# First product by row tiles, adapters with transposes three units behind and y's parts taken from PSUM

## The chip, the cores and the metric

One core of a Trainium2 chip runs the whole kernel as one program. The metric is the device time of one execution in microseconds (us). A core has TensorE (PE), which multiplies and transposes into PSUM, VectorE (DVE), ScalarE (ACT), GpSimd (POOL), which has no operand in PSUM in this kernel, and SyncE (SP), whose queue issues the DMAs here. Each engine works its own instructions off in the order written; between engines semaphores order the work.

## The reference, cut

Four sequences x of 512 x 512, everything in float32. One attention block with a two-stage network, then three adapters in a row (L1, L2, L3); for every sequence b, `stream[b]` picks one of three weight sets.

```python
q, k, v = x @ Wq, x @ Wk, x @ Wv
attn_out = softmax(q @ k.T * V ** -0.5) @ v @ Wp + bp
cms = gelu(attn_out @ cW1 + cb1) @ cW2 + cb2 + one_hot(code)
mod = gelu(concat(attn_out, cms) @ mW1 + mb1) @ mW2 + mb2
x = clip(x + cms + mod, 0, 1)
for layer in (L1, L2, L3):
    h = gelu(x @ W_down[stream] + b_down[stream]) @ W_up[stream] + b_up[stream]
    y = x + h
    x = (y - mean(y)) / sqrt(var(y) + 1e-5) * gamma[stream] + beta[stream]
```

## The kernel before

**Precision.** An operand of a product is held in two parts: the high part is the float32 value rounded to fp32r by a copy, the low part is value minus high part, rounded too. A product of two such operands takes three matmuls (high x high, high x low, low x high). ScalarE makes high parts, VectorE low ones, as a rule.

**First product** (`product(J_G, ...)`, the first of TensorE's program). G = Wq Wk^T, so that the scores are (x G) x^T. Wq and Wk arrive transposed in four row tiles of 128 each, eight DMAs of 256 KB on SP (L374). ScalarE casts each tile (L820), VectorE subtracts (L1142). TensorE computes four banks m, and for each runs over the four row tiles k, three matmuls each: 48 of 128x512. Bank 0 waits for the split of each tile k. The finished banks are cast (L781) and subtracted (L1084) into `g_w`, which the second product (x G) reads, each of its banks over all four tiles of `g_w`. In between ScalarE casts x and VectorE subtracts (L790, L1094). After that come the value product, scores, softmax and the two-stage network, which aren't changed; beside them weights of the adapters are split piece by piece (L796, L1516) and stored to DRAM.

**Adapters.** Twelve units u: layer u // 4 of sequence u % 4. A unit is, on TensorE: down (`t_down_mm`, 24 matmuls: h^T, two banks m of 512), up (`t_up_mm`, 24 matmuls: four banks `UP[i]`, rows of the sequence in the partitions), and 16 transposes of 128x128 (`t_transpose`, L756) of the normalised z back to columns of the sequence. In between:

- ScalarE: `h_gelu` (L1038, from PSUM to `hf`) and the casts of h (L1043); `z_norm` (L1028, four tiles of z in place); `y_scale` (L1052, PSUM times gamma plus beta to `yf`) and four casts of `yf` to the high part of `yT` (L1057).
- VectorE: `h_lo` (L1426, two), `z_stats`: z = UP + res (L1446), bn_stats (L1452) and bn_aggr (L1458) for four row tiles, `factors` (L1420, minus mean times rstd), `y_lo` (L1471, four, `yf` minus high part).
- GpSimd: variance plus eps (L1534) and its power -0.5, rstd (L1536), then for units 0 to 7 the result in rows, z times gamma (L1543) plus beta (L1545), four tiles each, which is the residual `res` of unit u + 4.

TensorE's program is written by slots s: down(s), up(s-1), transposes(s-2). Unit u's down reads `yT` of unit u-4, so a unit's result has two slots to become an operand. PSUM has eight banks: four are `UP`, four hold by turns down results and transposes (`down_bank`, `tr_bank`). z has two buffers, and z of unit u may be overwritten when GpSimd has read it and TensorE has transposed it. Units from `FINE` = 10 take their statistics in halves, so that normalising begins after two tiles. `y0_to_rows(b)` (L696, 16 transposes) and `y0_rows` (L1415) bring each sequence's first residual into rows, in slots 0 to 2.

SP loads in the order of its program: down weights `wd` (1 MB, L478) and up weights `wu` (1 MB, L485) of a unit, ten columns `pp` of gamma, beta and bias for each unit (L492), gamma and beta broadcast to rows `bc` (L498, L499), which waits for GpSimd's results of the unit two before.

## Time and profile before

| | us |
|---|---|
| median of 3 runs | 1217.73 |
| lowest and highest | 1216.46, 1219.93 |
| the profiled execution | 1217.09 |
| its span (first to last instruction) | 1215.0 |

| engine | busy us | share of the span |
|---|---|---|
| TensorE matmul | 1183.5 | 97% |
| VectorE | 808.1 | 67% |
| ScalarE | 565.2 | 47% |
| GpSimd | 173.3 | 14% |

GpSimd works only in about the first and the last sixth of the span. The trace gives for an instruction its start and its duration; a 128x512 matmul is listed with about 390 ns, but the next starts 227 ns after it, since they are pipelined. So a row of n matmuls covers about n x 0.227 plus the rest of the last one. "Idle before" in brackets is how long the engine had nothing, and whose instruction ended that. An interval that is spoken of as a slot goes from the first matmul of one down to the next.

### The profile page before, as it was taken

What the parts mean: (1) busy time and instruction counts of PE and PEld (TensorE: products, weight loads), DVE (VectorE), ACT (ScalarE), POOL (GpSimd) and SP (SyncE); (2) the same over time, 40 slices, a digit from 0 to 9 for tenths busy, and PEclk for the clock granted to TensorE, in tenths of its full rate; (3) what the DMA queues carried; (4) which work ended last, traced back from release to release, by engine and by line L of the source; (5) the groups of instructions that cost most, each with busy time, mean ns of one, the idle gap of its engine ahead of it and who ended that gap; (6) DMA issues with size and microseconds to landing.
All of it is one profiled execution on the core that took longest, in us unless ns stands there. A gap on an engine that the chain in (4) does not pass through costs nothing.

```text
span 1215.0 us, 15228 instructions
## 1 busy us (share of the span) xinstructions
PE 1183.5 (97%) x5312; PEld 974.9 (80%) x5312; DVE 808.1 (67%) x1461; ACT 565.2 (47%) x1068; POOL 173.3 (14%) x147
## 2 busy tenths in 40 slices
PE   7999999999999999999999999999999999999987
PEld 5888888788888788888888888878888888788776
DVE  5444395666668656565667776786665656889886
ACT  5344353563544534342435643454343343466666
POOL 1332230000000000000000000000000000578871
PEclk9999999999999999999999999999999999999999
DMA  5755452114320203020551311411111119655544
GB/s 192 266 205 174 165 178 104 53 46 162 122 96 35 96 1 104 4 101 14 201 237 52 131 61 35 174 53 52 53 52 53 52 48 364 229 168 181 175 150 162
DMA packets 51186, 145.82 MB, mean 120 GB/s; under 512 B 6420, under 2 KB 6420, under 8 KB 46886
## 3 DMA queue, kind: packets, MB, share of 16 engines
q1 hardware_dynamic: 51110, 144.84, 33.9%
q8 instruction: 43, 0.70, 0.2%
q14 instruction: 33, 0.27, 0.1%
HBM read 108.11 MB, written 36.71 MB: 119 GB/s over the span
## 4 chain that ended last, share of the span: by engine, by line
PE 79%; POOL 8%; DVE 6%; ACT 3%; issue 3%; DMA 1%; SPq 0%; POOLq 0%; ACTq 0%; DVEq 0%
PE psum L549 78%; POOL res L1543 3%; POOL res L1545 3%; ACT z L1028 1%; POOL sm L1536 1%; DVE sm L1452 1%; DVE res L1335 1%; DMA wk_raw<-wts_dram 1%; DVE res L1280 1%; ACT ring L885 0%; DVE ring L1199 0%; PE psum L756 0%; PE psum L583 0%; DVE z L1446 0%; DVE c_op L1307 0%
## 5 line engine op out<-in xcount | busy, mean ns | idle before, releaser
L549 PE MATMUL psum<-g_hl,w_hl 128*128 128x512 f32 x1536 | 351.4, 389 | 0.5 <-DVE w_hl L1258 0.4
L549 PEld LDWEIGHTS psum<-g_hl,w_hl 128*128 128x128 f32 x1536 | 288.2, 188 | 61.0 <-DVE w_hl L1258 0.8
L549 PE MATMUL psum<-a_op,ring 128*128 128x512 f32 x1344 | 319.0, 391 | 6.6 <-DVE w_t L1239 6.1
L549 PEld LDWEIGHTS psum<-a_op,ring 128*128 128x128 f32 x1344 | 253.2, 189 | 60.9 <-DVE w_t L1239 7.3
L549 PE MATMUL psum<-c_op,ring 128*128 128x512 f32 x672 | 165.1, 392 | 0.6 <-DVE c_op L1307 0.6
L549 PEld LDWEIGHTS psum<-c_op,ring 128*128 128x128 f32 x672 | 126.9, 189 | 28.4 <-DVE c_op L1307 2.0
L885 ACT CAST ring<-asum 128x256 fp32r<-128x256 f32 x192 | 76.6, 403 | 123.3 <-PE psum L549 90.8
L1524 POOL TENSOR_TENSOR yT<-res,yT 128x512 fp32r<-128x512 f32 x8 | 11.7, 1488 | 854.9 <-ACT yT L1023 854.9
L1265 DVE TENSOR_TENSOR g_hl<-g,g_hl 128x512 fp32r<-128x512 f32 x128 | 88.3, 690 | 67.1 <-ACT g_hl L925 65.3
L902 ACT ACTIVATE g<-g,sm 128x512 f32<-128x512 f32 x96 | 69.6, 725 | 120.8 <-DVE g L1245 52.3
L1199 DVE TENSOR_TENSOR ring<-asum,ring 128x256 fp32r<-128x256 f32 x192 | 80.7, 422 | 65.7 <-ACT ring L885 63.8
L925 ACT CAST g_hl<-g 128x512 fp32r<-128x512 f32 x128 | 78.3, 618 | 76.7 <-PE psum L549 76.7
L1199 DVE TENSOR_TENSOR ring<-rawp,ring 128x256 fp32r<-128x256 f32 x144 | 60.7, 423 | 75.2 <-ACT ring L885 74.9
L1280 DVE TENSOR_TENSOR res<-psum,res 128x512 f32<-128x512 f32 x96 | 64.9, 691 | 20.5 <-PE psum L549 20.5
L885 ACT CAST ring<-rawp 128x256 fp32r<-128x256 f32 x144 | 56.7, 403 | 43.0 <-PE psum L549 43.0
L549 PE MATMUL psum<-yT,wd 128*128 128x512 f32 x288 | 68.6, 393 | 6.1 <-issue 6.1
L1516 POOL TENSOR_TENSOR prep<-prep 128x512 f32<-128x512 f32 x36 | 51.2, 1428 | 129.9 <-ACT prep L796 129.9
L549 PEld LDWEIGHTS psum<-yT,wd 128*128 128x128 f32 x288 | 53.1, 188 | 18.0 <-issue 7.3
L549 PE MATMUL psum<-wu,h_hl 128*128 128x512 f32 x288 | 67.4, 390 | 0.0
L549 PEld LDWEIGHTS psum<-wu,h_hl 128*128 128x128 f32 x288 | 54.0, 188 | 11.2
L1258 DVE TENSOR_TENSOR w_hl<-wraw,w_hl 128x512 fp32r<-128x512 f32 x64 | 44.0, 688 | 20.3 <-ACT w_hl L916 19.4
L1028 ACT ACTIVATE z<-z,sm 128x512 f32<-128x512 f32 x46 | 33.9, 809 | 37.8 <-DVE sm L1420 37.8
(124 smaller groups left out, 1385.4 us busy)
## 6 DMA issues: line engine op xcount, KB each, us to landing
rawp<-up_w_dram SPq DMA_DIRECT2D x48, 512.0 KB, 3.5
wdu_split<-prep SPq DMA_DIRECT2D x36, 512.0 KB, 2.9
wraw<-dn_w_dram SPq DMA_DIRECT2D x64, 256.0 KB, 3.0
wd<-wdu_split SPq DMA_DIRECT2D x12, 1024.0 KB, 7.4
wu<-wdu_split SPq DMA_DIRECT2D x12, 1024.0 KB, 5.5
prep<-wdu_dram SPq DMA_DIRECT2D x36, 256.0 KB, 3.3
second_pair_operands<-c_op SPq DMA_DIRECT2D x7, 1024.0 KB, 7.0
a_op<-second_pair_operands SPq DMA_DIRECT2D x7, 1024.0 KB, 11.7
```

What stands on the lines that cost most here:

```text
L549: ins = nc.tensor.matmul(ps, lw(el), rw(er), start=first and i == 0, stop=last and i == 2, skip_group_check=skip)
L885: nc.scalar.copy(ring[n % RING][:, 0, :], aop_src(n)).then_inc(aop_hi, 1)
L902: nc.scalar.activation(dst, src, ACT.Gelu, bias=(cb1, mb1)[l][:, t:t + 1]).then_inc(gelu_done, 1)
L925: nc.scalar.copy(g_hl[t % GHL][:, 0, :], g[:, q, 2 * row + seq, :]).then_inc(g_hi_done, 1)
L1028: nc.scalar.activation(z[u % 2][:, i, :], z[u % 2][:, i, :], ACT.Identity, scale=rstd[:, u % 2, i:i + 1], bias=nmr[:, u % 2, i:i + 1]).the ...
L1199: nc.vector.tensor_tensor(ring[n % RING][:, 1, :], aop_src(n), f(ring[n % RING][:, 0, :]), ALU.subtract).then_inc(aop_lo, 1)
L1258: nc.vector.tensor_tensor(w_hl[t % 2][:, 1, :], wraw[t % 2][:, :], f(w_hl[t % 2][:, 0, :]), ALU.subtract).then_inc(w_lo_done, 1)
L1265: nc.vector.tensor_tensor(g_hl[t % GHL][:, 1, :], g[:, q, 2 * row + seq, :], f(g_hl[t % GHL][:, 0, :]), ALU.subtract).then_inc(g_lo_done, 1)
L1280: nc.vector.tensor_tensor(dst, bank[4 * seq + m], dst, ALU.add).then_inc(d_evac, 1)
L1516: nc.gpsimd.tensor_tensor(prep[i][:, 1, :], prep[i][:, 1, :], prep[i][:, 0, :], ALU.subtract).then_inc(p_lo, 1)
L1543: nc.gpsimd.tensor_tensor(res[:, u % B, i, :], z[i2][:, i, :], bc[i2][:, 0, :], ALU.mult).then_inc(t_rmul, 1)
L1545: nc.gpsimd.tensor_tensor(res[:, u % B, i, :], res[:, u % B, i, :], bc[i2][:, 1, :], ALU.add).then_inc(t_res, 1)
```

## The change

1. *First product.* It is taken by row tiles: for each k first high x high for all four banks, as soon as both casts are done, then the two mixed products for all four banks, after the subtracts. Ahead of it stand 16 transposes of the identity into a bank that isn't in use (`WARM`). Wq and Wk come in one array, a row tile of both in one DMA, four of 512 KB.
2. *Order of the adapters.* A slot is down(s), transposes(s-3), up(s-1). z gets a third buffer. The transposes' first two banks are `UP[2]` and `UP[3]`, so the up product's last two banks wait for VectorE's reading of them.
3. *y's parts.* ScalarE writes the high part straight from PSUM, rounded(scale x PSUM + beta) (`y_split`). VectorE computes scale x PSUM - high into `yf` (`y_less_high`, an input in PSUM and one in SBUF), and ScalarE adds beta and writes the low part. Before, it was scale, cast, subtract.
4. *Orders.* ScalarE: gelu, y's parts, casts of h, norms. VectorE: y, factors, then statistics with the two `h_lo` between them. GpSimd: two multiplies and an add of the rows of unit s-3, rstd of unit s-2, the other five row operations. `FINE` is 11, so unit 10 isn't taken in halves any more; for unit 11 VectorE normalises tiles 1 and 3.
5. *Loads.* The columns of all twelve units are loaded once before the adapters, and a unit's up weights directly behind its down weights.

The core of the diff, with the rest of the same kind left out:

```diff
-        z = [at("z0", 104, [P, DT, V]), at("z1", 136, [P, DT, V])]
+        z = [at(f"z{i}", k, [P, DT, V]) for i, k in enumerate((104, 136, 128))]
...
-            return bank[4 + 2 * ((u % 2) ^ (1 if d < 2 else 0)) + d % 2]
+            if u == 10:
+                return bank[4 + d]
+            return UP[2 + d] if d < 2 else bank[4 + 2 * (u % 2) + d - 2]
...
-        FINE = 10
+        FINE = 11
...
             for k in range(DT):
-                for i, w in enumerate((wq_raw, wk_raw)):
-                    sp.dma_start(w[:, k, :], wts[2 + i, :, k, :]).then_inc(s_wqk[i][k], 16)
+                sp.dma_start(wqk_raw[:, k, :, :], wqk[k]).then_inc(s_wqk[k], 16)
...
-            def unit_columns(u, layer, b):
-                if u >= B:
-                    sp.wait_ge(t_yf, (u - 4) * DT + DT)
-                row = layer * EXPERTS + ex[b]
-                sp.dma_start(pp[:, b, :], pp_all[bass.ds(row, 1)].rearrange("o p n -> (o p) n")).then_inc(t_pp[b], 16)
+            def unit_columns(u):
+                row = u // B * EXPERTS + ex[u % B]
+                sp.dma_start(pp[:, u, :], pp_all[bass.ds(row, 1)].rearrange("o p n -> (o p) n")).then_inc(t_pp, 16)
...
                     unit_down(u)
-                    if u >= B:
-                        unit_columns(u, u // B, u % B)
+                    unit_up(u)
                 if 4 <= u < 10:
                     unit_rows(u - 2, (u - 2) // B, (u - 2) % B)
-                if u < 12:
-                    unit_up(u)
...
-            product(J_G, HIGH, wqT, wkT, ready=split(qk_split, 0, per_k=2), free=known)
+            def product_by_pieces():
+                for k in range(DT):
+                    pe.wait_ge(qk_hi, 2 * k + 2)
+                    for m in range(DT):
+                        nc.tensor.matmul(bank[HIGH + m], wqT[:, 0, k, m * P:(m + 1) * P], wkT[:, 0, k, :], start=k == 0, stop=False)
+                    pe.wait_ge(qk_split, 2 * k + 2)
+                    for m in range(DT):
+                        for el, er in ((0, 1), (1, 0)):
+                            ins = nc.tensor.matmul(bank[HIGH + m], wqT[:, el, k, m * P:(m + 1) * P], wkT[:, er, k, :],
+                                                   start=False, stop=k == DT - 1 and el == 1)
+                        if k == DT - 1:
+                            ins.then_inc(bank_full, 1)
+            pe.wait_ge(s_ident, 1)
+            for i in range(WARM):
+                nc.tensor.transpose(bank[LOW][:, i % DT * P:(i % DT + 1) * P], ident[:, :], ident[:, :])
+            product_by_pieces()
...
+                    if u >= 2 and i >= 2:
+                        pe.wait_ge(t_yf, (u - 2) * DT + i - 1)
...
             y0_to_rows(0)
-            for s in range(14):
+            for s in range(15):
                 if s < 12:
                     t_down_mm(s, s % B)
                 if s == 0:
                     y0_to_rows(1)
+                if 3 <= s:
+                    t_transpose(s - 3, (s - 3) % B)
                 if 1 <= s < 13:
                     t_up_mm(s - 1, (s - 1) % B)
                 if 1 <= s < 3:
                     y0_to_rows(s + 1)
-                if 2 <= s:
-                    t_transpose(s - 2, (s - 2) % B)
...
+            def y_split(u):
+                for d in range(DT):
+                    act.wait_ge(t_tr, u * DT + d + 1)
+                    nc.scalar.activation(yT[u % B][:, 0, d, :], tr_bank(u, d), ACT.Identity,
+                                         scale=pp[:, u, d:d + 1], bias=pp[:, u, 4 + d:5 + d]).then_inc(t_yhi, 1)
+                for d in range(DT):
+                    act.wait_ge(t_yf, u * DT + d + 1)
+                    nc.scalar.activation(yT[u % B][:, 1, d, :], yf[d][:, :], ACT.Identity,
+                                         bias=pp[:, u, 4 + d:5 + d]).then_inc(t_ylo, 1)
...
             y0_hi(2)
-            for s in range(12):
-                if 2 <= s < 11:
-                    z_norm(s - 2)
-                h_gelu(s)
-                if s == 11:
-                    z_norm(9)
+            for s in range(14):
+                if s < 12:
+                    h_gelu(s)
+                if 3 <= s < 11:
+                    y_split(s - 3)
+                if 11 <= s:
+                    y_scale(s - 3)
+                if s < 12:
+                    h_hi(s)
                 if s == 0:
                     y0_hi(3)
                 if 2 <= s:
-                    y_scale(s - 2)
-            z_norm(10)
-            y_scale(10)
-            z_norm(11, (0, 2))
+                    z_norm(s - 2)
             y_scale(11, LAST_BY[0])
...
+                    if between is not None and i in (1, 3):
+                        between(i // 2)
                 if u >= FINE:
+                    norm_tile(u, 1)
                     factors(u, 2, 2)
-                else:
-                    factors(u, 0, DT)
-            def y_lo(u):
+                    norm_tile(u, 3)
+            def y_less_high(u):
                 for d in range(DT):
                     dve.wait_ge(t_yhi, u * DT + d + 1)
-                    nc.vector.tensor_tensor(yT[u % B][:, 1, d, :], yf[d][:, :], f(yT[u % B][:, 0, d, :]), ALU.subtract).then_inc(t_ylo, 1)
+                    if u >= 1:
+                        dve.wait_ge(t_ylo, (u - 1) * DT + d + 1)
+                    nc.vector.scalar_tensor_tensor(out=yf[d][:, :], in0=tr_bank(u, d), scalar=pp[:, u, d:d + 1], in1=f(yT[u % B][:, 0, d, :]),
+                                                   op0=ALU.mult, op1=ALU.subtract).then_inc(t_yf, 1)
...
             for s in range(13):
-                if s < 12:
-                    h_lo(s)
+                if 3 <= s < 11:
+                    y_less_high(s - 3)
+                if 2 <= s:
+                    factors(s - 2, 0, DT)
                 if s == 0:
+                    h_lo(0, 0)
+                    h_lo(0, 1)
                     y0_rows(1)
-                if 1 <= s < 13:
-                    z_stats(s - 1)
+                if 1 <= s:
+                    z_stats(s - 1, None if s == 12 else lambda m: h_lo(s, m))
                 if 1 <= s < 3:
                     y0_rows(s + 1)
-                if 2 <= s < 10:
-                    y_lo(s - 2)
-            norm_tile(3)
...
+            def rows_scaled(u, i):
+                if i == 0:
+                    pool.wait_ge(t_bc[u % 2], 32 * (u // 2 + 1))
+                z_ready(pool, u, i)
+                nc.gpsimd.tensor_tensor(res[:, u % B, i, :], z[u % 3][:, i, :], bc[u % 2][:, 0, :], ALU.mult).then_inc(t_rmul, 1)
+            def rows_shifted(u, i):
+                pool.wait_ge(t_rmul, u * DT + i + 1)
+                nc.gpsimd.tensor_tensor(res[:, u % B, i, :], res[:, u % B, i, :], bc[u % 2][:, 1, :], ALU.add).then_inc(t_res, 1)
+            for s in range(14):
+                if 3 <= s < 11:
+                    rows_scaled(s - 3, 0)
+                    rows_scaled(s - 3, 1)
+                    rows_shifted(s - 3, 0)
+                if 2 <= s:
+                    rstd_of(s - 2)
+                if 3 <= s < 11:
+                    rows_scaled(s - 3, 2)
+                    rows_shifted(s - 3, 1)
+                    rows_scaled(s - 3, 3)
+                    rows_shifted(s - 3, 2)
+                    rows_shifted(s - 3, 3)```

TensorE at the start of the program, before, from its first instruction (matmuls of Wq and Wk, then of x and G, then of Wv and Wp):

```order
L549 MATMUL psum<-wkT,wqT 128x512 x48
L549 MATMUL psum<-xT,g_w 128x512 x48
L549 MATMUL psum<-wp_s,wvT 128x512 x48
L549 MATMUL psum<-xT,uT 128x512 x48
L549 MATMUL psum<-vp_w,xT 128x512 x36
```

The same place now (L604 is high x high, L608 the mixed products):

```order
L616 MATMUL psum<-ident 128x128 x16
L604 MATMUL psum<-wkT,wqT 128x512 x4
L608 MATMUL psum<-wkT,wqT 128x512 x8
L604 MATMUL psum<-wkT,wqT 128x512 x4
L608 MATMUL psum<-wkT,wqT 128x512 x8
```

One row of 48 has become four pairs of 4 and 8 behind the 16 transposes; two of the pairs are shown.

VectorE at the end of slot 9 and the start of slot 10, before: factors of unit 8, y of unit 7 (`yT` from `yf`), h of unit 10, statistics of unit 9:

```order
L1420 SCALAR_TENSOR_TENSOR sm<-sm 128x4
L1471 TENSOR_TENSOR yT_116<-yf_120,yT_116 128x512
L1471 TENSOR_TENSOR yT_116<-yf_121,yT_116 128x512
L1471 TENSOR_TENSOR yT_116<-yf_122,yT_116 128x512
L1471 TENSOR_TENSOR yT_116<-yf_123,yT_116 128x512
L1426 TENSOR_TENSOR h_hl_128<-hf_132,h_hl_128 128x512
L1426 TENSOR_TENSOR h_hl_128<-hf_133,h_hl_128 128x512
L1446 TENSOR_TENSOR z_127<-psum,res 128x512 x2
L1452 BN_STATS sm<-z_127 128x6
L1446 TENSOR_TENSOR z_127<-psum,res 128x512
L1452 BN_STATS sm<-z_127 128x6
```

The same work now, in slot 10, from the third y subtract of unit 7 on:

```order
L1496 SCALAR_TENSOR_TENSOR yf_121<-psum,unit_columns,yT_115 128x512
L1496 SCALAR_TENSOR_TENSOR yf_122<-psum,unit_columns,yT_115 128x512
L1445 SCALAR_TENSOR_TENSOR sm<-sm 128x4
L1469 TENSOR_TENSOR z_125<-psum,res 128x512 x2
L1475 BN_STATS sm<-z_125 128x6
L1450 TENSOR_TENSOR h_hl_128<-hf_132,h_hl_128 128x512
L1469 TENSOR_TENSOR z_125<-psum,res 128x512
L1475 BN_STATS sm<-z_125 128x6
L1481 BN_AGGR sm<-sm 128x2
L1469 TENSOR_TENSOR z_125<-psum,res 128x512
L1475 BN_STATS sm<-z_125 128x6
L1481 BN_AGGR sm<-sm 128x2
```

The y subtracts read PSUM and come ahead of the factors, and the two h subtracts, which stood together ahead of the statistics, stand among them; the second one follows the rows shown.

GpSimd in one slot before (L1534 and L1536 variance and power, L1543 and L1545 the rows' multiply and add; the z's number tells the unit's buffer):

```order
L1534 TENSOR_SCALAR sm<-sm 128x4
L1536 TENSOR_TENSOR sm<-sm 128x4
L1543 TENSOR_TENSOR res<-z_127,bc_131 128x512
L1545 TENSOR_TENSOR res<-res,bc_131 128x512
L1543 TENSOR_TENSOR res<-z_127,bc_131 128x512
```

And now:

```order
L1569 TENSOR_TENSOR res<-z_126,bc_131 128x512 x2
L1573 TENSOR_TENSOR res<-res,bc_131 128x512
L1560 TENSOR_SCALAR sm<-sm 128x4
L1562 TENSOR_TENSOR sm<-sm 128x4
L1569 TENSOR_TENSOR res<-z_126,bc_131 128x512
L1573 TENSOR_TENSOR res<-res,bc_131 128x512
L1569 TENSOR_TENSOR res<-z_126,bc_131 128x512
L1573 TENSOR_TENSOR res<-res,bc_131 128x512 x2
```

The power no longer precedes the rows of its own unit; it stands between the third and the fourth row operation of the unit before.

## Rows read from the trace of the kernel before

**Rows 1.** The page: busy time, share, instructions; the chain by engine.

```profile
PE 1183.5 (97%) x5312; PEld 974.9 (80%) x5312; DVE 808.1 (67%) x1461; ACT 565.2 (47%) x1068; POOL 173.3 (14%) x147
...
PE 79%; POOL 8%; DVE 6%; ACT 3%; issue 3%; DMA 1%; SPq 0%; POOLq 0%; ACTq 0%; DVEq 0%
```

**Rows 2.** Timeline, first 32 us: start, duration, engine, line, tiles [idle before, releaser].

```profile
6.29 1.65 PE L549 MATMUL psum<-wkT,wqT 128*128 128x512 f32 x3 [6.29 <-DVE wkT L1142]
...
11.53 0.69 DVE L1142 TENSOR_TENSOR wkT<-wk_raw,wkT 128x512 fp32r<-128x512 f32 x1
...
14.02 2.50 DVE L1094 TENSOR_TENSOR xT<-res,xT 128x512 fp32r<-128x512 f32 x4 [1.80 <-ACT xT L790]
```

**Rows 3.** Timeline of TensorE alone, 10.9 to 13.5 us, and 16 to 21.

```profile
10.93 2.99 PE L549 MATMUL psum<-wkT,wqT 128*128 128x512 f32 x6 [0.34 <-DVE wkT L1142]
...
15.75 5.61 PE L549 MATMUL psum<-wkT,wqT 128*128 128x512 f32 x24
```

**Rows 4.** Timeline, 22 to 75 us.

```profile
22.10 11.04 PE L549 MATMUL psum<-xT,g_w 128*128 128x512 f32 x48
22.30 0.59 ACT L781 CAST g_w<-psum 128x512 fp32r<-128x512 f32 x1 [2.13 <-PE psum L549]
...
22.92 0.69 DVE L1084 TENSOR_TENSOR g_w<-psum,g_w 128x512 fp32r<-128x512 f32 x1 [2.03 <-ACT g_w L781]
...
53.40 0.68 ACT L801 ACTIVATE probs<-psum,sm 128x512 f32<-128x512 f32 x1
...
54.74 8.33 PE L549 MATMUL psum<-vp_w,xT 128*128 128x512 f32 x36
```

**Rows 5.** Busy time by engine in windows: slot 7, and slot 11 to the end.

```profile
1126.13:1140.84 14.71, 13.30 (x64) 10.68 (x65) 13.21 (x20) 9.86 (x17) 13.04 (x11) 1.00 0.51 179
...
1184.97:1211.57 26.60, 23.57 (x120) 19.79 (x120) 19.49 (x47) 18.59 (x27) 5.03 (x10) 0.95 0.39 151
```

The columns of these rows are PE, PEld, DVE, ACT and POOL busy with their instructions, granted clock, DMA share, GB/s.

**Rows 6.** Timeline, slots 6 and 7 (1100 to 1136 us).

```profile
1111.41 5.72 PE L549 MATMUL psum<-yT,wd 128*128 128x512 f32 x24 [0.61 <-issue]
...
1120.05 0.17 DVE L1420 SCALAR_TENSOR_TENSOR sm<-sm 128x4 f32<-128x4 f32 x1 [1.46 <-POOL sm L1536]
...
1120.25 2.93 ACT L1028 ACTIVATE z<-z,sm 128x512 f32<-128x512 f32 x4 [4.87 <-DVE sm L1420]
1121.21 1.36 POOL L1543 TENSOR_TENSOR res<-z,bc 128x512 f32<-128x512 f32 x1 [1.20 <-ACT z L1028]
...
1126.13 5.72 PE L549 MATMUL psum<-yT,wd 128*128 128x512 f32 x24 [1.09 <-issue]
```

**Rows 7.** Groups by shape, 1072 to 1186 us: busy us, mean ns | idle before.

```profile
L1471 DVE TENSOR_TENSOR yT<-yf,yT 128x512 fp32r<-128x512 f32 x32 | 34.2, 1130 | 0.0
L1426 DVE TENSOR_TENSOR h_hl<-hf,h_hl 128x512 fp32r<-128x512 f32 x16 | 24.3, 1559 | 4.2 <-ACT h_hl L1043 3.8
L1446 DVE TENSOR_TENSOR z<-psum,res 128x512 f32<-128x512 f32 x30 | 19.5, 670 | 0.0
...
L1028 ACT ACTIVATE z<-z,sm 128x512 f32<-128x512 f32 x32 | 23.5, 807 | 29.8 <-DVE sm L1420 29.8
L1052 ACT ACTIVATE yf<-psum,sm 128x512 f32<-128x512 f32 x32 | 22.2, 776 | 10.6 <-PE psum L756 10.6
L1057 ACT CAST yT<-yf 128x512 fp32r<-128x512 f32 x32 | 17.5, 634 | 0.0
```

**Rows 8.** SP's timeline, and the page's DMA issues (KB each, us to landing).

```profile
1110.03 0.60 SPq L478 DMA_DIRECT2D wd<-wdu_split  x1
...
wd<-wdu_split SPq DMA_DIRECT2D x12, 1024.0 KB, 7.4
```

**Rows 9.** Timeline, 1184 us to the end.

```profile
1200.11 1.29 DVE L1446 TENSOR_TENSOR z<-psum,res 128x512 f32<-128x512 f32 x2
...
1203.15 1.91 PE L756 MATMUL psum<-ident,z 128*128 128x128 f32 x16
...
1207.41 0.41 PE L756 MATMUL psum<-ident,z 128*128 128x128 f32 x2 [2.36 <-ACT z L1028]
```

127 lines of the change are left out of this document (58 added, 69 removed).

## The prediction

> **What bounds the kernel now.** Read first the page's busy shares and the chain that ended last [rows 1]: TensorE is busy 97% of the span and holds 79% of the chain, so only places where it waits, or runs at the lower clock, can give time. The chain's 8% of GpSimd says where the largest of them is. Then the two stretches that the change touches, in order of time.
>
> *The first product.* TensorE's first three matmuls start at 6.29, as soon as row tile 0 of both weights is split, but the next nine wait for tiles 1 to 3, because bank 0 wants all four tiles before bank 1 may begin; the last split is issued at 11.53 [rows 2]. Six matmuls around 11 us take 2.99 us, 24 later ones take 5.61 [rows 3]. Less the 0.39 of the last one's own latency the second is 0.227 us apiece, the 2.4 GHz level; the first is near 0.43, the 1.2 GHz level. The second product starts at 22.10 [rows 4]. So 36 of the 48 matmuls are run after everything has landed.
>
> *The adapters.* In the ask for equal windows a unit takes 14.71 us, of which TensorE is credited 13.3 [rows 5]. Its dense work is less: 48 matmuls x 0.227 = 10.9, and 16 transposes, 1.91 for all less the last one's latency, 1.75 [rows 9]: 12.65. Five units (slots 6 to 10, one window of five is shown) run at 14.71; slots 3 to 5 run dense, and slot 6 opens with 0.6 of idle [rows 6]. What ends the wait is a ring through GpSimd: VectorE waits 1.46 for rstd, ScalarE normalises, GpSimd's first row operation starts after ScalarE's first tile (1121.21, idle 1.20), eight row operations follow, and only then the next rstd [rows 6]. GpSimd is busy 13.04 of 14.71 with eleven operations, VectorE 13.2 [rows 5]. Both are stretched by each other: VectorE's subtracts with two SBUF inputs take 1130 and 1559 ns on average, the add that has one input in PSUM 670 on the same 128x512 [rows 7].
>
> **The change part by part.**
>
> *First product by row tiles.* 48 matmuls stay 48; 16 warm transposes of the identity go in front (the identity is written by about 1.5 us, and they are idle work: nothing reads them). High x high of tile 0 can start when both casts are done, one VectorE operation of 0.69 [rows 2] before the start shown: 5.6. Dense from there at 2.4 GHz the product ends at 5.6 + 10.9 = 16.5. Tile 3 is wanted only after 40 matmuls (14.7), and is split at 12.2, so landings don't bind unless they are 2.5 us later than now; the weights go in four DMAs of twice the size, the same bytes. If the clock stays low for the first 4 matmuls, add 0.8: 17.3. If it rises no earlier than now (about 14), the 40 matmuls left at 11 cost 2 us more: 18.9. The trace shows the lower clock while TensorE had worked in short pieces, and the higher one after it had worked without a break from 10.93 [rows 3]; transposes from 1.5 to about 5 and matmuls from 5.6 are such work earlier, so I take 17.3.
> [...]
>
> What follows doesn't shift by the full 4.8. All four banks now close within 1.4 us, and cast (0.59) and subtract (0.69) of four tiles [rows 4] queue: the second product's first bank wants the last of them. Four subtracts from 16.5 or so (x's own split ends at 16.5, [rows 2]) with the last bank's cast done at 18.7: last subtract 19.8, first bank closed at 20.5. Before: 22.10 + 12 x 0.227 = 24.8. **Gain 4.3**; ends 2.3 (clock late) and 4.9 (nothing late). Is it kept? The value product starts at 54.74 with no wait, after an exponential begun at 53.40 [rows 4] has freed its bank at 54.0, so there is 0.7 to 1.3 of slack, and ScalarE there is paced by weight pieces whose first store waits behind the sum of the betas, which itself follows these subtracts and moves with them. I keep all 4.3, with 2 as the lower bound.
>
> *Transposes three units behind.* Before, slot s is down(s), up(s-1), transposes(s-2). Now it is down(s), transposes(s-3), up(s-1). One set (1.75) leaves the stretch ahead of down(3) and comes back behind down(11): **-1.7** here, and its return is in the tail.
>
> *y's parts from PSUM, other orders.* VectorE's four subtracts (two SBUF inputs, 1130 ns) become four with in0 in PSUM, nearest to the add of [rows 7]: 670, pitch 0.60. GpSimd no longer meets them; its row operation unhindered is 1.36 [rows 6], and eight are at pitch 1.25 to 1.38, 10.4, with 0.4 for each of the two h subtracts that still meet it, and 1.4 for variance and power: 12.6. ScalarE swaps four casts (634) for four activations (807): 4 x (807 + 776 + 807) + four short ones at 0.65, less 0.1 overlap each: about 11 [rows 7]. All three are now under or at TensorE's 12.65. The ring is cut: GpSimd starts with rows of a unit normalised a slot earlier, and rstd sits in their middle.
>
> But order, not sums, decides, so I lay one slot out from its down's start, with durations from [rows 6, 7]. ScalarE: gelu 0 at 3.0, gelu 1 at 5.75, four high parts 6.4 to 9.1, four low parts to 12.0, h's two casts to 13.1, four norms to 16.0 (next gelu at 15.7: 0.3 late, harmless, as gelu 1 is due only at 18.4). VectorE: y subtracts 7.1 to 9.8, z adds from 10, first h subtract 12.6 to 14.2 (it waits for ScalarE's cast, and behind it stand two z adds, three stats and the second h subtract), second h subtract to 18.4, done at 19.3; next y subtract at 19.8. GpSimd: three row operations from 13.9, rstd at 19.3 (idle 1.0), done 20.8, five more to 27.4, i.e. 2.1 into the slot after next. There are two loops here. Second h subtract, gelu 1, high parts, low parts, casts, first h subtract, adds, second h subtract: 12.4 to 12.7. GpSimd: 12.6. TensorE: 12.65. Three loops that near give a little more than the largest: I take 12.8, bounds 12.65 and 13.6. Slots 3 to 10 before: 3 x 12.65 + 0.6 + 5 x 14.71 = 112.1; after 8 x 12.8 = 102.4: **-9.7**, bounds -10.9 and -3.3.
>
> *SP.* The load of down(u+1) now stands behind the row loads of unit u-2, as before, but those wait for GpSimd's rows of u-4, which end 2.1 into slot u: issued at 3.0, landed 7.4 us later [rows 8] at 10.4, wanted at 12.65. Before it was issued at 1110.03 for 1126.13 [rows 6, 8], 16 us ahead. Cover 2.2 us, cost nothing while it holds. The twelve column loads ahead of unit 0's up weights are issued while the last chunk's matmuls run; nothing. The column loads leaving the loop free SP: nothing.
>
> *The tail.* From down(11)'s start to the last transpose is 26.6 now [rows 5]. After: down 5.45, transposes 1.75, up(10) 5.45 = 12.65; VectorE then still has an add, three statistics and an h subtract: 15.5. Unit 10 is no longer done in halves, so VectorE stands 1.5 for rstd [rows 6] with unit 11's adds queued behind it: they begin at 17.1, where they now begin at 1200.11 - 1184.97 = 15.1 [rows 9]. ScalarE's scaling of unit 10 adds 0.2. **+2.2**. Now TensorE idles 2.36 before the last transposes [rows 9], and will again idle 2 to 3, so the clock loss there stays.
>
> Sum: -4.3 - 1.7 - 9.7 + 2.2 = -13.5, from the profiled execution's 1217.1 (span 1215.0 and 2.1 around it): **1203.6**. The median shown is 0.6 above that execution; I leave that in the range.
>
> **The rivals.**
> 1. *The VectorE-ScalarE loop sets the slot.* Each h subtract stands alone among GpSimd's operations; if each waits out a whole one (1.3) and then runs 0.65, it is 1.95 for the mean of 1.56: loop up to 13.5, with another ragged 0.1 13.6: 8 x 0.8 = +6.4, 1210.0. For: the 1559 mean. Against: GpSimd idles 1.0 just there. The Trainium skill (SBUF — State Buffer, "SBUF: two separate sides") has the pair locked for a whole instruction and the loser fully blocked, which speaks for this rival.
> 2. *Down weights late.* If landing plus GpSimd's lag grow by 3.2 us, 1 us per slot for down(5) to down(10): +6, 1209.6. Against: 2.2 us of cover.
> 3. *The head's gain is lost* before the adapters (the bank freed at 54.0 comes late, or the clock): 0 to 2 kept, 1205.9 to 1207.9.
> 4. *Slower.* The new y subtracts, which read one SBUF tensor, meet GpSimd all the same. At 1.56 each the loop is 12.4 + 4 x 0.96 = 16.2, 8 slots 129.6: +17.5 - 4.3 - 1.7 + 2.2 = +13.7, 1230.8. It decides from (112.1 + 3.8) / 8 = 14.5 per slot, a subtract of 1.1 us. Against: 30 adds of that form average 670 with GpSimd busy throughout.
>
> **How the numbers follow.** Forecast 0.62 (1199 to 1207); rival 1 0.13; rival 2 0.08; rival 3 0.09; rival 4 0.04; something I don't see that takes most of the gain back 0.04. The range runs from all terms at their good end (-4.9 - 1.7 - 10.9 + 2.2 = -15.3, and some short waits in slots 1 and 2 that I left out, 1199.5) to rivals 1 and 2: 1199 to 1211, leaving out about 0.15. Within 0.3% of before, about what a measurement can tell, means above 1214.1: faster 0.92, same 0.04, slower 0.04.
>
> **What would show it.** Second product from about 17.4 with its first bank closed near 20.5, and everything to 1030 shifted by 4. A slot of 12.8 with no TensorE wait over 0.2. y subtracts at 0.67, row operations mostly under 1.4. Unit 11's adds 17 us after down(11). Wrong if a slot is over 13.2: then look who is last, the low parts (rival 1), wd landings (rival 2) or y subtracts over 1 us (rival 4).

## The result and the profile after

| | before | after |
|---|---|---|
| median (4 runs each, same chip) | 1217.10 us | 1202.83 us |
| lowest and highest | 1215.34, 1219.93 | 1201.54, 1203.89 |
| the profiled execution | 1217.09 (span 1215.0) | 1201.54 (span 1199.8) |

The ratio is 0.988, with a 95% interval of 0.9858 to 0.9902: faster by 1.2%, 14.3 us by the medians. The prediction was 1203.6 with a range of 1199.0 to 1211.0, and it held.

The page of after, the same two lines as [rows 1]: busy time by engine, and the chain that ended last by engine.

```profile
PE 1180.3 (98%) x5328; PEld 974.9 (81%) x5328; DVE 788.1 (66%) x1460; ACT 568.8 (47%) x1068; POOL 161.2 (13%) x145
...
PE 86%; DVE 6%; DMA 2%; ACT 2%; issue 2%; POOL 1%; SPq 0%; POOLq 0%; DVEq 0%; ACTq 0%
```

GpSimd's share of the chain fell from 8% to 1%, and TensorE's rose from 79% to 86%: the ring through rstd is no longer what ended last.

**The head.** The timeline of after, first 20 us (start, duration, engine, line, tiles, and in brackets the idle time before and who ended it), answers to [rows 2 to 4]:

```profile
1.52 3.53 PE L616 MATMUL psum<-ident 128*128 128x128 f32 x16 [1.52 <-POOL ident L1530]
...
5.65 1.19 PE L604 MATMUL psum<-wkT,wqT 128*128 128x512 f32 x4 [0.60 <-ACT wkT L841]
...
6.68 2.00 PE L608 MATMUL psum<-wkT,wqT 128*128 128x512 f32 x8
...
10.76 2.18 ACT L811 CAST xT<-res 128x512 fp32r<-128x512 f32 x4 [1.35 <-DMA res<-x_dram]
...
14.86 1.97 PE L608 MATMUL psum<-wkT,wqT 128*128 128x512 f32 x8
...
15.51 2.06 ACT L802 CAST g_w<-psum 128x512 fp32r<-128x512 f32 x4 [2.57 <-PE psum L608]
16.13 2.48 DVE L1109 TENSOR_TENSOR g_w<-psum,g_w 128x512 fp32r<-128x512 f32 x4 [2.23 <-ACT g_w L802]
```

The first four matmuls of Wq and Wk take 1.19 us, less the last one's latency about 0.25 each, nearly the 2.4 GHz pitch from the first on. From there the product is dense, and the second product starts at 16.97 (before 22.10). The value product starts at 49.70 (54.74) and down(0) at 1029.95 (1035.29).

**The adapters.** Busy time in windows, in the columns of [rows 5]: slot 8 (from 0.11 us ahead of its first matmul to 0.10 short of its end; [rows 5] had slot 7), and slot 11 to the end.

```profile
1128.94:1141.60 12.66, 12.66 (x66) 10.72 (x65) 10.09 (x20) 10.35 (x17) 11.72 (x10) 1.00 0.59 209
1167.03:1197.00 29.97, 25.63 (x137) 21.49 (x135) 19.49 (x45) 22.26 (x32) 4.46 (x8) 0.94 0.41 157
```

TensorE is busy for all of the 12.66 us, where it had 13.30 of 14.71. VectorE went from 13.2 to 10.1 and GpSimd from 13.0 to 11.7. The groups by shape, 1070 to 1178 us, answer to [rows 7]:

```profile
L1573 POOL TENSOR_TENSOR res<-res,bc 128x512 f32<-128x512 f32 x31 | 43.0, 1400 | 0.0
...
L1569 POOL TENSOR_TENSOR res<-z,bc 128x512 f32<-128x512 f32 x29 | 37.3, 1295 | 8.7 <-ACT z L1049 8.7
...
L1469 DVE TENSOR_TENSOR z<-psum,res 128x512 f32<-128x512 f32 x34 | 22.3, 673 | 3.5 <-PE psum L557 3.5
...
L1496 DVE SCALAR_TENSOR_TENSOR yf<-psum,unit_columns,yT 128x512 f32<-128x512 f32 x32 | 22.1, 751 | 20.2 <-ACT yT L1072 20.2
L1076 ACT ACTIVATE yT<-yf,unit_columns 128x512 fp32r<-128x512 f32 x32 | 20.6, 734 | 0.0
...
L1450 DVE TENSOR_TENSOR h_hl<-hf,h_hl 128x512 fp32r<-128x512 f32 x16 | 15.7, 981 | 1.0 <-ACT h_hl L1066 0.3
```

The y subtract costs 751 ns where it cost 1130, the h subtract 981 where it cost 1559, and the z add is what it was (673, 670). VectorE now waits for work 20.2 us in this stretch, for ScalarE's high parts. How slot 8 goes is seen in the timeline, 1129 to 1142 us (part of what [rows 6] showed of before):

```profile
1129.05 5.61 PE L557 MATMUL psum<-yT,wd 128*128 128x512 f32 x24
...
1129.72 2.56 POOL L1569 TENSOR_TENSOR res<-z,bc 128x512 f32<-128x512 f32 x2 [0.80 <-ACT z L1049]
...
1131.37 0.62 SPq L490 DMA_DIRECT2D wd<-wdu_split  x1
...
1134.06 0.19 POOL L1560 TENSOR_SCALAR sm<-sm 128x4 f32<-128x4 f32 x1
...
1134.50 1.91 PE L777 MATMUL psum<-ident,z 128*128 128x128 f32 x16
...
1136.09 2.76 DVE L1496 SCALAR_TENSOR_TENSOR yf<-psum,unit_columns,yT 128x512 f32<-128x512 f32 x4 [2.45 <-ACT yT L1072]
...
1141.05 1.13 DVE L1450 TENSOR_TENSOR h_hl<-hf,h_hl 128x512 fp32r<-128x512 f32 x1
```

TensorE has no idle time over 0.1 between the start of down(3) and 1179. GpSimd waits 0.80 once in a slot, for the first normalised tile, and rstd (1134.06) stands in the middle of its rows.

**The tail.** The timeline of after, 1178 to 1197 us, answers to [rows 9]:

```profile
1179.72 0.66 PE L777 MATMUL psum<-ident,z 128*128 128x128 f32 x4
...
1180.98 1.53 PE L777 MATMUL psum<-ident,z 128*128 128x128 f32 x12 [0.60 <-DVE z L1469]
...
1184.41 0.16 DVE L1445 SCALAR_TENSOR_TENSOR sm<-sm 128x4 f32<-128x4 f32 x1 [1.41 <-POOL sm L1562]
1184.52 1.48 DVE L1469 TENSOR_TENSOR z<-psum,res 128x512 f32<-128x512 f32 x2
...
1192.10 0.41 PE L777 MATMUL psum<-ident,z 128*128 128x128 f32 x2 [2.36 <-ACT z L1049]
...
1193.18 3.11 PE L777 MATMUL psum<-ident,z 128*128 128x128 f32 x14 [0.67 <-ACT z L1049]
```

VectorE stands 1.41 us for unit 10's rstd with unit 11's adds behind it, which begin 17.5 after down(11)'s start at 1167.03. The wait of 0.60 inside unit 9's transposes was not there before.

Summed up by where the time is in the two profiled executions, in us:

| stretch | before | after | difference | forecast |
|---|---|---|---|---|
| start to down(0) | 1035.29 | 1029.95 | -5.34 | -4.3 |
| down(0) to down(3) | 37.28 | 35.61 | -1.67 | -1.7 |
| down(3) to down(11), 8 slots | 112.40 | 101.47 | -10.93 | -9.7 |
| down(11) to the last transposes' end | 26.60 | 29.26 | +2.66 | +2.2 |
| sum | | | -15.28 | -13.5 |

The differences are those of one execution of each kernel. How far one execution can be trusted for the first line is taken up below.

### The profile page after: what moved, and what is told of

Same layout as the page of the kernel before. It is cut to its first block, busy times and chain, and to the rows that moved or that the text cites. A ratio compares the mean times of both kernels' runs of the same rounds, so it can differ in the third digit from the quotient of the medians.

```text
span 1199.8 us, 15272 instructions
## 1 busy us (share of the span) xinstructions
PE 1180.3 (98%) x5328; PEld 974.9 (81%) x5328; DVE 788.1 (66%) x1460; ACT 568.8 (47%) x1068; POOL 161.2 (13%) x145
## 4 chain that ended last, share of the span: by engine, by line
PE 86%; DVE 6%; DMA 2%; ACT 2%; issue 2%; POOL 1%; SPq 0%; POOLq 0%; DVEq 0%; ACTq 0%
PE psum L557 83%; DMA prep<-wdu_dram 2%; PE psum L777 2%; POOL prep L1543 1%; DVE c_op L1332 1%; DVE res L1360 1%; DVE res L1305 1%; DVE ring L1224 1%; PE psum L608 0%; ACT ring L906 0%; ACT prep L817 0%; PE psum L721 0%; PE psum L604 0%; DMA wqk_raw<-wqk_dram 0%; DVE sm L1475 0%
## 5 line engine op out<-in xcount | busy, mean ns | idle before, releaser
L557 PE MATMUL psum<-g_hl,w_hl 128*128 128x512 f32 x1536 | 351.4, 389 | 0.5 <-DVE w_hl L1283 0.4
L557 PEld LDWEIGHTS psum<-g_hl,w_hl 128*128 128x128 f32 x1536 | 288.1, 188 | 61.2 <-DVE w_hl L1283 0.8
L557 PE MATMUL psum<-a_op,ring 128*128 128x512 f32 x1344 | 318.5, 390 | 6.7 <-DVE w_t L1264 6.1
L557 PEld LDWEIGHTS psum<-a_op,ring 128*128 128x128 f32 x1344 | 252.7, 188 | 60.8 <-DVE w_t L1264 7.4
L557 PE MATMUL psum<-c_op,ring 128*128 128x512 f32 x672 | 163.9, 390 | 0.7 <-DVE c_op L1332 0.6
L557 PEld LDWEIGHTS psum<-c_op,ring 128*128 128x128 f32 x672 | 126.0, 188 | 28.6 <-DVE c_op L1332 2.5
L1305 DVE TENSOR_TENSOR res<-psum,res 128x512 f32<-128x512 f32 x96 | 64.8, 691 | 20.5 <-PE psum L557 20.5
L557 PE MATMUL psum<-wu,h_hl 128*128 128x512 f32 x288 | 68.4, 393 | 0.0
L557 PE MATMUL psum<-yT,wd 128*128 128x512 f32 x288 | 67.8, 391 | 0.0
L1543 POOL TENSOR_TENSOR prep<-prep 128x512 f32<-128x512 f32 x36 | 49.0, 1366 | 128.0 <-ACT prep L817 128.0
L557 PEld LDWEIGHTS psum<-yT,wd 128*128 128x128 f32 x288 | 53.7, 188 | 11.2
L557 PEld LDWEIGHTS psum<-wu,h_hl 128*128 128x128 f32 x288 | 53.3, 188 | 10.7
L930 ACT COPY u_t<-psum 128x512 f32<-128x512 f32 x32 | 18.9, 590 | 61.6 <-PE psum L557 61.6
## 6 DMA issues: line engine op xcount, KB each, us to landing
wd<-wdu_split SPq DMA_DIRECT2D x12, 1024.0 KB, 9.6
wu<-wdu_split SPq DMA_DIRECT2D x12, 1024.0 KB, 5.4
second_pair_operands<-c_op SPq DMA_DIRECT2D x7, 1024.0 KB, 6.7
a_op<-second_pair_operands SPq DMA_DIRECT2D x7, 1024.0 KB, 12.6
```

Of the source, the lines that this page charges most:

```text
L557: ins = nc.tensor.matmul(ps, lw(el), rw(er), start=first and i == 0, stop=last and i == 2, skip_group_check=skip)
L930: nc.scalar.copy(u_t[:, :], bank[4 * q + BANK_OF[P1]]).then_inc(u_done, 1)
L1305: nc.vector.tensor_tensor(dst, bank[4 * seq + m], dst, ALU.add).then_inc(d_evac, 1)
L1543: nc.gpsimd.tensor_tensor(prep[i][:, 1, :], prep[i][:, 1, :], prep[i][:, 0, :], ALU.subtract).then_inc(p_lo, 1)
```

## The experiments

"Head" means the stretch up to the second product. The theory after the result: the head's gain comes from the order of the matmuls, the adapters' from cutting the ring and from taking one input of VectorE's y subtract out of SBUF, where it met GpSimd's operations, and the two gains add. The rivals: the gain of the adapters belongs to the order alone or to y's parts alone, the head's to the warm transposes or to the four loads, and one half's gain is lost without the other.

### Head alone, adapters alone

The kernel before with the product by row tiles, the new loads and the warm transposes; and the kernel after with the old `product(J_G, ...)`, eight loads and no warm transposes.

> The kernel before with only the first product changed (row tiles, four loads of both weights, 16 warm transposes). Theory A (the two halves of the change add up): the adapters' slots stay as before, 14.7 us for slots 6 to 10, and the whole is 5.0 to 5.4 us shorter than before, since the changed kernel's first adapter product started 5.34 us earlier; 1211.7. Theory B (the 5.3 us are in part owed to the adapters' new order, for instance by the columns' loads): under 4 us, over 1213.

> The changed kernel with the first product, its eight loads and no warm transposes as before. Theory A: first adapter product at 1035.3 as before, slots 3 to 10 at 12.7 us, 9.9 us shorter than before (1.67 + 10.93 - 2.66), 1207.2. Theory B: the rest, so over 10.5 or under 9.

Head alone: 1212.35, ratio 0.9964 (0.9953 to 0.9975), 4.7 less than the 1217.04 of before on that chip, a little under the 5.0 to 5.4 expected; by the interval it is 3.0 to 5.7 less. Its slots are the old 14.7, and it shows the second product at 17.01. Adapters alone: 1206.04, 0.9913 (0.9897 to 0.9929), 11.0 less, which by the letter of the expectation is its theory B. Its slots 3 to 10 take 101.44, as in the kernel after. 4.7 + 11.0 = 15.7 against 14.3 for both: they add, inside the intervals. From down(0) to the end its trace is 9.9 shorter than before's (169.9 against 179.8), which is what theory A asked for; the rest lies ahead of down(0), which starts at 1034.39, 0.9 earlier than before. In that stretch only the source of its eight loads differs from before (its last weight subtract starts at 10.33, before's at 11.53, and x's first cast at 12.19 instead of 13.37), but its matmuls also ran 0.23 us apart from 9.98 on, where before's around 11 were still 0.43 apart. Whether the 0.9 is the source's or that execution's, one trace can't tell.

### What in the head gives the time

```diff
-WARM = 16
+WARM = 0
```

> The changed kernel without the 16 warm transposes. Theory W (they bring the clock up before the first product): the first matmuls of the product are 0.43 us apart, the clock rises only after some 3 to 8 us of the product's own work, and the second product starts 1 to 3 us later than 16.97. Theory V (the product's own pieces would bring it up in time, the transposes do nothing): the second product at 17.0 to 17.9.

The kernel before with 16 transposes of the identity ahead of the old product:

> The kernel before with only the 16 warm transposes ahead of its first product. Theory W: the first product's pieces at 6.3, 8.9 and 10.9 are then at 0.23 us and the second product starts at 12.28 + 39 x 0.227 = 21.1 in place of 22.1, 1 us earlier, because the old order waits for the last tile anyway. Theory V: no change, 22.1. If the clock falls back in the waits between the pieces, also 22.1, and the traces of the two kernels show it by the distance of the matmuls.

The kernel after with eight loads of 256 KB instead of four, from the new array:

```diff
-                sp.dma_start(wqk_raw[:, k, :, :], wqk[k]).then_inc(s_wqk[k], 16)
+                for i in range(2):
+                    sp.dma_start(wqk_raw[:, k, i, :], wqk[k, :, i, :]).then_inc(s_wqk2[i][k], 16)
```

> The changed kernel with the two weights in eight loads of 256 KB as before (2 KB in a row) in place of four of 512 KB. Theory L (the larger loads brought tiles and x earlier): the last split of the weights goes from 9.5 back towards 11.5, x's cast from 10.8 towards 13.4, and the second product starts later than 16.97 by up to 1 us since x's own split stands ahead of the subtracts that it needs. Theory M (only TensorE's own order counted): the second product at 17.0.

The kernel after with the array laid out otherwise, four loads:

```diff
-                sp.dma_start(wqk_raw[:, k, :, :], wqk[k]).then_inc(s_wqk[k], 16)
+                sp.dma_start(wqk_raw[:, k, :, :], wqk[:, k]).then_inc(s_wqk[k], 16)
```

> The changed kernel with its four loads of Wq and Wk taken from an array in which the rows of one row tile lie 16 KB apart (4 KB read, 12 KB skipped), as the two arrays of before had them 8 KB apart, where the changed kernel reads a row tile as one block of 512 KB. Theory L, the layout in DRAM is what let x and the last weight tiles land earlier than before (x's first cast at 10.76 against 13.37): x's cast comes back to 12.0 to 13.5, the second product still starts at 17.0 to 17.3, but its first bank waits up to 1 us for g_w's last subtract, and the value product starts at 50.0 to 50.8 instead of 49.7. Theory N, the layout is nothing: x's cast at 10.6 to 11.0, value product at 49.7.

Without the transposes: 1203.63, 0.9899 (0.9881 to 0.9917); the first matmuls on TensorE's timeline:

```profile
5.58 2.05 PE L604 MATMUL psum<-wkT,wqT 128*128 128x512 f32 x4 [5.58 <-ACT wkT L841]
7.43 2.67 PE L608 MATMUL psum<-wkT,wqT 128*128 128x512 f32 x8
9.94 1.07 PE L604 MATMUL psum<-wkT,wqT 128*128 128x512 f32 x4
```

The first four take 1.85 us and the next eight 2.51: about seven of the twelve are at the 1.2 GHz pitch (0.43), up to about 9.0, and all later ones at the 2.4 GHz one (0.227). The second product starts at 18.40, 1.43 later than in the kernel after. That looks like the worth of the transposes. But the kernel with the other array layout shows this, and one with the same head from the next group is like it:

```profile
1.52 3.67 PE L616 MATMUL psum<-ident 128*128 128x128 f32 x16 [1.52 <-POOL ident L1530]
...
6.08 2.07 PE L604 MATMUL psum<-wkT,wqT 128*128 128x512 f32 x4 [0.89 <-ACT wkT L841]
...
7.95 2.85 PE L608 MATMUL psum<-wkT,wqT 128*128 128x512 f32 x8
...
11.35 2.18 ACT L811 CAST xT<-res 128x512 fp32r<-128x512 f32 x4 [1.34 <-DMA res<-x_dram]
```

The transposes ran, and the clock was low all the same until about 9.8: the eight matmuls from 7.95 take 2.69 up to the next group at 10.64, which is four at 0.43 and four at 0.23. All the kernels that were profiled with this head or with one piece of it changed, by their own timelines (one execution each):

```
                  first matmul   4 take  next 8   second product   value product   down(0)
after                5.65         1.19    2.00       16.97            49.70        1029.95
eight loads          5.17         1.43    1.98       16.71            49.47        1030.88
head alone           5.70         1.19    1.99       17.01            49.74        1030.93
tail (below)         5.65         1.38    2.00       17.16            49.92        1030.14
two behind (below)   5.60         1.69    1.98       17.39            50.14        1031.52
old y (below)        5.74         2.07    3.16       19.07            51.83        1031.60
other layout         6.08         2.07    2.85       19.13            51.89        1031.12
no transposes        5.58         2.05    2.67       18.40            51.16        1030.62
```

"Old y" and "after" have the same instructions up to here and begin their matmuls within 0.1 us of each other; one has the high clock and the other not. With the transposes the clock had risen by about 6.7 in five of seven executions, and rose at about 9.8 and 10.1 in two, later than the 9.0 of the kernel without them. The Trainium skill (TensorE: Matmul & The Clock Gate, "What's actually happening") says that the point at which the clock rises varies from run to run of one kernel; this table agrees. Nor does the difference last: the spread of 2.4 us at the value product is 1.65 at down(0), with the kernel without transposes 0.7 behind the kernel after, and the intervals of the two kernels overlap. The windows 390 to 406, after and without transposes, show where a part of it goes:

```profile
390.00:406.00 16.00, 13.39 (x53) 10.66 (x52) 12.83 (x27) 8.19 (x17) 0.00 (x0) 0.89 0.26 94
390.00:406.00 16.00, 13.30 (x57) 10.28 (x56) 13.60 (x27) 7.32 (x15) 0.00 (x0) 1.00 0.28 99
```

In the kernel after the granted clock is 0.50 from 393.9 to 397.3. The three executions whose clock rose late in this head (no transposes, other layout, old y) have no such low stretch between the value product and down(0), and take 979.2 to 979.8 us from one to the other; the five with one take 980.2 to 981.4; the four with two, of which before is one, take 980.6 to 982.7. No edit touches this stretch. So an early rise was followed by a low stretch in the middle that gave a part of its gain back; why, no run shows. And the down(0) of a single execution says nothing of differences under some 2 us.

The transposes alone on the kernel before gave 1216.44 in a single execution (before's own lie between 1214.7 and 1220.1), with pieces at 6.19 (3 in 1.65) and 8.85 (6 in 3.01) still at the low clock; TensorE waits about a microsecond ahead of each. That execution shows no gain. What carries the head's gain is the order by row tiles: the second product starts at 16.7 to 19.1 in all eight kernels that have it, and at 20.1 to 22.4 in the four with the old order. It is shown by taking away the transposes, the larger loads and the layout one at a time; the order with all three as before was not run.

The loads (single executions: 1202.49 with eight loads, 1202.78 with the other layout): with eight of them x's first cast is at 12.54 instead of 10.76, and SP issues x's load at 4.49 and not at 2.60. With eight loads from the two old arrays it is at 13.3 to 13.4 (three kernels), with eight from the new array at 12.19 and 12.54. With four loads it is at 10.7 to 10.9 in five kernels, at 11.35 in the one with the other layout, but also at 11.42 in the one without transposes, which has the block layout: so for four loads the layout's share isn't shown. With eight loads the second product still started at 16.71 with no wait in its first bank, and the value product 32.76 after it (32.73 in the kernel after): the loads didn't carry the time. Of the layout, its first cast 0.43 later may have cost the clock in that execution or not; a single one can't tell.

### What in the adapters gives the time

The order of after with y's parts as before (`y_split` writes `yf`, then casts; VectorE subtracts in SBUF):

```diff
-                    nc.vector.scalar_tensor_tensor(out=yf[d][:, :], in0=tr_bank(u, d), scalar=pp[:, u, d:d + 1], in1=f(yT[u % B][:, 0, d, :]),
-                                                   op0=ALU.mult, op1=ALU.subtract).then_inc(t_yf, 1)
+                    nc.vector.tensor_tensor(yT[u % B][:, 1, d, :], yf[d][:, :], f(yT[u % B][:, 0, d, :]), ALU.subtract).then_inc(t_ylo, 1)
```

> The changed kernel, all its orders kept, but y's parts as before: ScalarE scales PSUM into yf and casts it, VectorE subtracts two SBUF tensors. Theory O (the order was the lever, the meeting of VectorE and GpSimd a side matter): slots 3 to 10 stay within 0.1 us of 12.68, total within 1 us of the changed kernel. Theory P (both are needed): each of the four subtracts waits out a GpSimd operation, 1.1 to 1.8 us instead of 0.75, the slot grows to 13.2 to 14.2 and the total by 4 to 12 us.

The kernel before with y's parts from PSUM, everything else in the old order (VectorE's new subtract stands where the old one stood, after the statistics and factors; ScalarE's low parts, which wait for it, stand a slot later, after the gelu):

> The kernel before, slot order and FINE as before, with y's parts from PSUM; ScalarE's low parts stand one slot later, after the gelu. Theory O: the ring through GpSimd stays, GpSimd's eight row operations shrink from about 12.1 to 10.6 us, so slots 6 to 10 go from 14.71 to about 13.3 and the total falls by 5 to 7 us. Theory P2 (the meeting was the lever): the slot falls to TensorE's 12.65 in the old order too, total 10 us less. No change would mean that the ring is made of waits and not of GpSimd's durations.

The kernel after with TensorE's slot and the transposes' banks as before; ScalarE takes y's parts ahead of gelu, VectorE's order stays:

```diff
+                if 1 <= s < 13:
+                    t_up_mm(s - 1, (s - 1) % B)
...
-                if 3 <= s:
-                    t_transpose(s - 3, (s - 3) % B)
-                if 1 <= s < 13:
-                    t_up_mm(s - 1, (s - 1) % B)
+                if 2 <= s:
+                    t_transpose(s - 2, (s - 2) % B)
```

> The changed kernel, with TensorE's order of a slot put back to down(s), up(s-1), transposes(s-2) and the transposes' banks as before; y's parts from PSUM, the third z buffer and the orders on VectorE and GpSimd stay, and ScalarE takes y's parts ahead of gelu, since down(s) now waits for them. Theory T, the move of the transposes by a slot is what gives the chain its time: laid out from the start of down(s), down's first bank waits for the last unit's y subtract in PSUM (about 1 us after the last transpose), and the norms of unit s-2 must end by 10.9 instead of 18, while their rstd comes only at about 5 and the four norms stand on ScalarE behind y's parts, gelu and the casts, to about 12: slots 3 to 10 take 13.8 to 15.5 each, 1212 to 1225 in all. Theory U, the orders on VectorE, ScalarE and GpSimd do it alone: slots of 12.7 to 13.0, within 3 us of the changed kernel's 1202.8.

*New order, old y*: 1226.24, ratio 1.0069 (1.0052 to 1.0085), slower than before, and 23 us over the kernel after where 4 to 12 were expected. Slots from 6 on take 16.4 each, not 13.2 to 14.2. Its groups, 1107 to 1189 us, and rows of its timeline around the start of slot 7 (1123.80):

```profile
L1495 DVE TENSOR_TENSOR yT<-yf,yT 128x512 fp32r<-128x512 f32 x22 | 34.7, 1634 | 19.1 <-ACT yT L1078 19.1
L557 PE MATMUL psum<-yT,wd 128*128 128x512 f32 x120 | 32.4, 405 | 10.0 <-DVE yT L1495 10.0
L1567 POOL TENSOR_TENSOR res<-z,bc 128x512 f32<-128x512 f32 x21 | 31.9, 1532 | 8.1 <-ACT z L1049 8.1
```

```profile
1122.18 6.35 DVE L1495 TENSOR_TENSOR yT<-yf,yT 128x512 fp32r<-128x512 f32 x4 [3.18 <-ACT yT L1078]
...
1128.45 0.15 DVE L1446 SCALAR_TENSOR_TENSOR sm<-sm 128x4 f32<-128x4 f32 x1
1128.53 1.27 DVE L1470 TENSOR_TENSOR z<-psum,res 128x512 f32<-128x512 f32 x2
...
1128.59 3.69 PE L557 MATMUL psum<-yT,wd 128*128 128x512 f32 x15 [0.73 <-DVE yT L1495]
```

Four subtracts last 6.35 us, each waiting out a GpSimd operation, and they stand ahead of the factors, the adds and the h subtracts. The down product waits for them directly.

*Old order, new y*: 1256.48, 1.0317 (1.03 to 1.0334). Slots of about 19. GpSimd's operations are short now, 1.29 in the row below, and the slot is the longest of all (timeline, 1133 to 1136 us):

```profile
1133.73 2.73 DVE L1475 SCALAR_TENSOR_TENSOR yf<-psum,sm,yT 128x512 f32<-128x512 f32 x4
1133.85 2.93 ACT L1028 ACTIVATE z<-z,sm 128x512 f32<-128x512 f32 x4 [1.62 <-DVE sm L1422]
1134.58 7.21 PE L549 MATMUL psum<-yT,wd 128*128 128x512 f32 x24 [3.88 <-issue]
1134.80 1.29 POOL L1548 TENSOR_TENSOR res<-z,bc 128x512 f32<-128x512 f32 x1 [1.19 <-ACT z L1028]
```

down(6) can't start before VectorE has read the transposes' first bank (0.75 of its 2.73), and VectorE reads it only after the statistics and the rstd of the next unit. TensorE idles 3.88, and its next 24 matmuls take 7.21 instead of 5.6, at a granted clock of 0.78 after 0.99 in the 11.6 us before them. My expectation had only counted durations.

*Transposes two units behind*: 1244.19, 1.0207 (1.019 to 1.0224). Slots of 17.7, longer than the 13.8 to 15.5 expected. Timeline, 1119 to 1127 us:

```profile
1119.70 1.75 DVE L1446 TENSOR_TENSOR h_hl<-hf,h_hl 128x512 fp32r<-128x512 f32 x1
...
1120.85 1.74 POOL L1569 TENSOR_TENSOR res<-res,bc 128x512 f32<-128x512 f32 x1
1121.02 1.91 PE L773 MATMUL psum<-ident,z 128*128 128x128 f32 x16
...
1123.91 0.65 DVE L1446 TENSOR_TENSOR h_hl<-hf,h_hl 128x512 fp32r<-128x512 f32 x1
...
1125.29 2.71 DVE L1492 SCALAR_TENSOR_TENSOR yf<-psum,unit_columns,yT 128x512 f32<-128x512 f32 x4
...
1126.13 7.30 PE L555 MATMUL psum<-yT,wd 128*128 128x512 f32 x24 [3.20 <-issue]
```

ScalarE makes the high parts from 1121.66 to 1124.4, but VectorE is in the adds, the second h subtract and the statistics until 1125.3, and the down product waits 3.20 for its bank, then runs 7.30 at a granted clock of 0.77. I had laid out ScalarE's queue for this run and not VectorE's. With the transposes a slot later and between two products, that same work of VectorE lies behind 5.5 us of up product.

So neither y's parts from PSUM nor the later transposes can be taken out of this change by itself. All together the adapters gain 10 to 11 us. Without y's parts from PSUM the kernel is 9 us over before, without the later transposes 26 (both with the head's 4.7 in it), and y's parts from PSUM without any of the orders are 39 over it. Not tried is the rival between them: transposes two behind, or the old order, with VectorE's subtract moved ahead of the statistics. So it isn't shown that the third unit is needed as such, only that it is with VectorE's orders as they are. The orders on VectorE, ScalarE and GpSimd, `FINE` and the loads of the adapters weren't taken away one at a time either.

### The tail

Unit 9's transposes into banks 4 to 7 like unit 10's, so that they don't wait for `UP[2]` and `UP[3]`; and the factors of unit 10 behind the first of unit 11's adds.

```diff
-            if u == 10:
+            if u >= 9:
                 return bank[4 + d]
...
                 for i in range(DT + 2):
+                    if u == 11 and i == 1:
+                        factors(10, 0, DT)
```

> The changed kernel with two waits of its end taken away: unit 9's transposes go to four banks that are free since unit 11's gelu, not to two that wait for unit 10's last adds, and VectorE does unit 10's factors after unit 11's first add, not ahead of it. Theory: the 0.76 us wait inside unit 9's transposes is gone, unit 11's adds begin 1 us earlier, and the distance from down(11) to the last transpose goes from 29.3 to about 28.2 us; total 1 us less, which three rounds can hardly tell. Rival: the end hangs on ScalarE (norms of unit 10, scaling of unit 10 ahead of the norms of unit 11), then it stays at 29.3.

1201.92, 0.9876 (0.9859 to 0.9892), the fastest of all, but its interval and that of the kernel after (0.9858 to 0.9902) don't separate them. TensorE's timeline:

```profile
1179.78 1.91 PE L780 MATMUL psum<-ident,z 128*128 128x128 f32 x16
...
1191.66 0.41 PE L780 MATMUL psum<-ident,z 128*128 128x128 f32 x2 [2.36 <-ACT z L1052]
1192.55 1.75 PE L780 MATMUL psum<-ident,z 128*128 128x128 f32 x14 [0.47 <-ACT z L1052]
```

The 0.60 is gone, and from down(11) (1167.13) to the end of the last transposes are 27.2 us instead of 29.3. Of these 2.1, 1.36 is that the last 14 transposes ran at the high clock (1.75 against 3.11). The kernel "head alone" has the same 1.75 with the old adapters, and the other ten traces have 2.7 to 3.3, so this part is luck of the execution. The other 0.7 is an add: unit 10's factors come 17.4 after down(11) in both kernels, and one add of unit 11 (0.69, at +16.2) now stands ahead of them. TensorE's wait of 0.60 isn't on that path: in the kernel after, unit 11's adds wait for rstd and not for their bank.

## Why the prediction was right, step by step

- **What bounds the kernel.** Right. With the ring through GpSimd cut, its part of the chain went from 8% to 1%, and TensorE is dense from down(3) to 1179.
- **First product, -4.3.** The mechanism was right. The term was 1.0 too small for these two executions (-5.3), while head alone, by its medians, gave 4.7 with 4.3 well inside its interval of 3.0 to 5.7. The second product started at 16.97 instead of 17.3. The step that was mis-sized is the one behind it, the last cast done at 18.7, the last subtract at 19.8 and the first bank closed at 20.5: the casts ran from 15.51 to 17.57, the four subtracts from 16.13 to 18.6, and no matmul waited. With four casts at 0.59 the 18.7 lets them begin at 16.3; the first one began at 15.51, while the other banks were still being computed. The other number there, x's split ended at 16.5, was off too (13.9), but the sum didn't hang on it, and the kernel with eight loads (x's split ended at 15.7, second product at 16.71) shows that the gain wasn't owed to x's landing. Against that, I took the clock's rise for a thing of the work ahead of it, with one answer (17.3); the table above has both ends, 16.7 and 19.1, for nearly the same start. The bounds of 2.3 and 4.9 can't be judged at down(0): against this execution of before (1035.29) the kernels with the new head give 3.7 to 5.3, but three others with the old head start it anywhere from 1034.4 to 1037.7.
- **Transposes three units behind, -1.7.** Right: 1.67. But the line that it filled was too small for what it does. The prediction spoke of it as a set that moves from here to there; the run with the transposes two behind shows that, with VectorE's orders as they are, it is a condition for the slot of 12.7.
- **y's parts and orders, -9.7.** 12.68 a slot against 12.8: -10.93, at the good bound. 0.9 of the 1.2 is the slot, 0.3 that the eight slots of before measured 112.4 and not 112.1. The y subtract was forecast at 0.67 and is 0.75. Rival 1's loop didn't bind, because the h subtract doesn't wait out a whole operation of GpSimd each time: 981 ns in the mean, not 1559 and not 1.95 us. The loop that I had at 12.4 to 12.7 with two of them at 1.56 is 1.2 shorter with that, and TensorE's own 12.65 is the bound.
- **SP, nothing.** Right, by less than I said. The load of the down weights was issued at 2.3 into the slot rather than 3.0, but takes 9.6 us in the middle instead of the 7.4 of [rows 8] (9.2 to 10.1 over four). It now follows up weights and row loads within 2 us; that this is the cause is likely, but no run takes it apart. It lands at 1140.9 for 1141.70, and for down(7) at 1116.1 for 1116.31: a cover of 0.8 and of 0.2, not 2.2. Rival 2 was nearer than its 0.08, and that it cost nothing was in part luck.
- **Tail, +2.2.** +2.7. The adds of unit 11 came at +17.5 instead of +17.1, for the reason given (VectorE stands 1.41 for rstd), since VectorE was done with unit 10 at +16.0 and not at +15.5. I had also missed the wait of 0.60 in unit 9's transposes: its first two banks are `UP[2]` and `UP[3]`, wanted while VectorE still adds unit 10 from them, with no up product between. It isn't on the path of unit 11's adds, so it doesn't explain the difference.
- **Rival 3** (head's gain lost) didn't happen: 5.13 at the second product, 5.04 at the value product, and 4.7 in the whole time of head alone.
- **Rival 4** (slower, y subtracts meeting GpSimd, a loop of 16.2) didn't happen, and its price for a slot was right. The kernel with the old subtracts in the new order has just this mechanism, at 1634 ns a subtract and 16.4 a slot, and came out slower than before, at 1226.2 and not 1230.8, since its slots 3 and 4 stayed at 12.8 and 12.7. The Trainium skill (SBUF — State Buffer, "SBUF: two separate sides") has a VectorE operation with two SBUF inputs and a GpSimd one exclude each other for a whole instruction. The rows agree on both sides: the same h subtract takes 0.65 when GpSimd is idle and 1.75 beside an operation of GpSimd, which in turn takes 1.74 and not 1.29; the y subtract with one input in PSUM takes 0.75 with GpSimd busy.

The sum was 1.8 short of the 15.28 of the profiled executions, with -1.0, -1.2 and +0.5 from the three terms, and 0.8 short of the 14.3 of the medians. The low end of the range, 1199, was not added up from the terms: they give 1201.8, and the 2.3 below it were put down to short waits in slots 1 and 2, which didn't shrink at all (down(0) to down(2) takes 21.82 before and 21.85 after).

## What to carry to other kernels

Cost an order by laying out one whole period with every engine's queue, as was done here for the new order; the two runs whose expectation left VectorE's queue out were wrong by 45 us and, from the upper end of what was expected, by 19 us. A reader of a PSUM bank that a product wants next has to stand early in its engine's queue, or the product waits for everything ahead of it, as it did in two kernels here: moving a subtract's input from SBUF to PSUM makes it shorter and at the same time gives it a bank to hold. Before an early start is credited with a higher clock, look at more than one execution.

## What the runs showed of the hardware

- The column of the granted clock reads 1.00 for the first 12 us in every one of these kernels, while matmuls in it run at 0.43 us apiece. There the level is to be read from the matmuls' pitch.
- With the same instructions and starts within 0.1 us, the first twelve matmuls took 3.0 us in one execution and 5.0 in another.
- The 16 transposes of the identity took 3.42 us in "head alone", with the last one 0.11 us behind the one ahead of it, where the others are 0.21 apart, the first two 0.27: the clock rose there at about 4.6, while TensorE had run nothing but transposes.
- 1 MB of down weights landed in 7.4 us in the queue order of before, and in 9.6 behind another MB and two row loads of 256 KB that were issued in the 2 us ahead.
